# Layer 0's scores and search in four 32-row quarters, each search pair inside the scores; expert stages by chunks

## The reference

```
x = x + tanh(g_xattn[0]) * L0_xattn(layernorm(x), ctx)
x = x + tanh(g_ffn[0])   * L0_ffn(layernorm(x))
x = x + tanh(g_xattn[1]) * L1_xattn(layernorm(x), ctx, mask)
x = x + tanh(g_ffn[1])   * L1_ffn(layernorm(x))

L0_xattn:  q = query @ Wq.T in 32 heads of 4;  k = ctx @ Wk.T likewise;  v = ctx @ Wv.T in 16 heads of 8
           a1, a2 = softmax(q1 k1^T / 2) v, softmax(q2 k2^T / 2) v      (heads 0-15 and 16-31)
           attn = a1 - lam * a2;  attn *= rsqrt(mean(attn^2) + 1e-5) * subln_w * (1 - LAMBDA_INIT)
           out = attn @ Wp.T + bp
L1_xattn:  the plain one, 16 heads of 8, with biases, masked scores set to the least float
L0_ffn:    softmax over 8 experts, the two best, weighted: silu(x @ w_up.T) @ w_down.T, plus a shared expert
L1_ffn:    the two best of 8, softmax over the two: (silu(h1) * h2) @ w3.T
```

## Time and profile before

| | |
|---|---|
| median of 3 runs | 2283.0 us (2277.94 to 2285.57) |
| the profiled execution | 2273.94 us, its span 2272.1 us |
| PE busy | 2036.9 us, 90% |
| DVE busy | 1702.4 us, 75% |
| ACT busy | 1497.4 us, 66% |
| POOL busy | 1273.1 us, 56% |
| exponentials of 896 columns, L1081 | 1152 of 915 ns |
| reductions of 500 keys, L1139 | 1536 of 672 ns |

### The profile page before, as it was taken

One profiled execution on the slowest core, in us unless ns is written; L12 is line 12 of the kernel. 1 busy time (PEld: TensorE's weight loads), 2 busy tenths in 40 slices (PEclk: granted clock), 3 DMA queues, 4 the chain that ended last, 5 costly groups with the idle time before them and its releaser, 6 DMA issues. The chain is left out here.

```text
span 2272.1 us, 67374 instructions
## 1 busy us (share of the span) xinstructions
PE 2036.9 (90%) x27256; PEld 1260.1 (55%) x27256; DVE 1702.4 (75%) x3701; ACT 1497.4 (66%) x2101; POOL 1273.1 (56%) x1418
## 2 busy tenths in 40 slices
PE   3799999999999999999985985999999999998798
PEld 2344444444444444444443863567766776676576
DVE  3688888888888888888943554777777777774644
ACT  2168888888888888888773432577777777776322
POOL 5326556556556556556423444687777778771332
PEclk9589999999999999999997996799999999999799
DMA  3544453453443443444301015677767777761000
GB/s 101 129 84 109 93 112 108 95 112 107 95 112 107 95 112 107 95 112 108 67 2 54 25 31 120 141 157 146 155 140 147 154 153 152 144 141 37 33 1 16
DMA packets 95244, 227.82 MB, mean 100 GB/s; under 512 B 46308, under 2 KB 58852, under 8 KB 88292
## 3 DMA queue, kind: packets, MB, share of 16 engines
q1 hardware_dynamic: 94692, 223.67, 44.2%
q10 hardware_dynamic: 256, 0.00, 0.0%
HBM read 146.77 MB, written 76.48 MB: 98 GB/s over the span
## 5 line engine op out<-in xcount | busy, mean ns | idle before, releaser
L1081 ACT ACTIVATE probs<-score_ps 125x896 f32<-125x896 f32 x1152 | 1039.0, 915 | 309.4 <-PE score_ps L978 304.7
L1139 DVE TENSOR_REDUCE max_part<-max_ps 112x1 f32<-112x500 f32 x1024 | 663.6, 672 | 81.8 <-PE max_ps L949 43.0
L995 PE MATMUL acc_ps<-probs,vext 125*32 125x224 f32 (+1 forms) x12288 | 563.4, 312 | 4.5 <-issue 3.7
L978 PE MATMUL score_ps<-qstack,kstack 50*125 50x224 f16 (+1 forms) x6144 | 456.2, 249 | 72.4 <-ACT probs L1081 67.1
L978 PEld LDWEIGHTS score_ps<-qstack,kstack 50*125 50x125 f16 x6144 | 305.5, 134 | 310.5 <-ACT probs L1081 246.5
L949 PE MATMUL max_ps<-kstack,qstack 48*112 48x500 f16 x1536 | 460.5, 394 | 17.8 <-DMA kstack<-k_parts 12.9
L995 PEld LDWEIGHTS acc_ps<-probs,vext 125*32 125x32 f32 x12288 | 303.4, 110 | 188.8 <-issue 136.3
L1136 DVE CUSTOM_DVE_ANT_0 kstack<-max_ps,kstack 112x500 f32<-112x500 f32 x512 | 333.4, 675 | 84.1 <-PE max_ps L949 56.0
L1139 DVE TENSOR_REDUCE max_part<-spare_ps 112x1 f32<-112x500 f32 x512 | 344.5, 673 | 44.6 <-PE max_ps L949 42.9
L949 PE MATMUL spare_ps<-kstack,qstack 48*112 48x500 f16 x768 | 304.4, 396 | 18.7 <-issue 16.8
L1136 DVE CUSTOM_DVE_ANT_0 kstack<-spare_ps,kstack 112x500 f32<-112x500 f32 x256 | 172.8, 675 | 83.9 <-PE max_ps L949 80.9
(11 more groups left out here) (187 smaller groups left out, 2617.5 us busy)
## 6 DMA issues: line engine op xcount, KB each, us to landing
kstack<-k_parts SPq DMA_DIRECT2D x384, 187.5 KB, 6.4
k_parts<-khl SPq DMA_DIRECT2D x128, 375.0 KB, 2.9
ctx_f<-in_ctx SPq DMA_DIRECT2D x32, 750.0 KB
ctx_f<-context_parts SPq DMA_DIRECT2D x22, 750.0 KB, 8.0
context_parts<-ctx_f SPq DMA_DIRECT2D x16, 750.0 KB, 3.3
context_parts<-kstack SPq DMA_DIRECT2D x16, 750.0 KB, 3.3
mask_in<-in_mask SPq DMA_DIRECT2D x128, 82.0 KB
XnT<-context_parts SPq DMA_DIRECT2D x10, 750.0 KB, 8.2
```

The costliest lines, as they stand in the source:

```text
L978: last = nc.tensor.matmul(buf[0:KT, r, GC * k:GC * (k + 1)], kstack[n % SLOTS][rows, c, keys], qstack[n % SLOTS][rows, c, :], start=not L. ...
L995: last = nc.tensor.matmul(acc_ps[32 * j:32 * j + 32, TT * S * i:TT * S * (i + 1)].rearrange("p (s c) -> p s c", s=S), vext[n % SLOTS][:, c ...
L1081: nc.scalar.activation(probs[t % 2][:, 896 * h:896 * h + 896].rearrange("k (b c) -> k b c", b=2), score_ps[h][0:KT, :, 0:448], ACT.Exp, sc ...
L1139: nc.vector.reduce_max(best, scores, AX.X).then_inc(s_red, 1)
```

## The change

Layer 0's stacks are four quarters of 32 partitions (`TILE`, `ROW_TILES`) with 8 dimensions to a group: 24 rows and the two of ones and maxima make 26. A matmul of `scores` takes 26 rows and gives 112 columns; place 0 uses two of the quarters and place 1 the other two. Search has 24 rows. `piece` orders the pairs so that each takes the two quarters that the scores beside it don't, and `scores` issues the pair ahead of its first matmul (`SEARCH_AT = 0`). Layer 0 has one order of a step. All DMAs that fill or load stacks in layer 0 are for each quarter, so twice as many. Layer 1 keeps its halves. In `feed_forward` the loop over chunks is written out, the router's matmuls are split around the first expert's hidden units, the choice of experts and its exponential come later, the total of chunk c-1 is added in chunk c, and layer 1's result is stored by chunk in the same block.

```diff
-L0 = Layer("L0", 32, 4, False)
-L1 = Layer("L1", 16, 8, True)
+L0 = Layer("L0", 32, 4, False, HALF // 2)
+L1 = Layer("L1", 16, 8, True, HALF)
...
-    CONST = 16 * (2 * SLOTS + (2 if L.masked else 0))
-    K_INC = 16 * 6
-    Q_INC = 16 * 6
-    M_INC = 16 * 4
+    CONST = 16 * (ROW_TILES * SLOTS + (2 if L.masked else 0))
+    K_INC = 16 * 3 * ROW_TILES
+    Q_INC = 16 * 3 * ROW_TILES
+    M_INC = 16 * 2 * ROW_TILES
+    SEARCH_AT = 0
...
-              "pairs apart by preparation": ("scores 0", "weigh", "scores 1", "pair 0", "prepare", "pair 1")}
+              "each search pair inside the scores": ("scores and pair 0", "weigh", "scores and pair 1", "prepare")}
     def order_of(n, t):
+        if not L.masked:
+            return ORDERS["each search pair inside the scores"]
...
     def piece(p):
-        r, third, c, i = p % 2, p // 2 % NTHIRD, p // (2 * NTHIRD) % PAIRS, p // (2 * NTHIRD * PAIRS)
-        return r, third, c, i, (r * PAIRS + c) * L.parts + i
+        if L.masked:
+            r, third, c = p % 2, p // 2 % NTHIRD, p // (2 * NTHIRD)
+        else:
+            turn = p // 4
+            r, third, c = 2 * (p // 2 % 2 ^ turn % 2) + p % 2, turn % NTHIRD, turn // NTHIRD
+        return r, third, c, r * PAIRS + c
...
             def fill_k(n):
                 at_least(sp, s_scores, (n - 2) * STEPS * 2)
                 for part, blocks in ((0, (0, 1)), (1, (2,))):
                     sp.wait_ge(s_kd[part], 16 * (n + 1))
                     for k in blocks:
-                        for r in range(2):
-                            row = HALF * r + GD * k
+                        for r in range(ROW_TILES):
+                            row = TILE * r + GD * k
                             sp.dma_start(kstack[n % SLOTS][row:row + GD, :, :],
-                                         T["k_dram"][n:n + 1, part, HALF * r:HALF * r + HALF, :]
+                                         T["k_dram"][n:n + 1, part, TILE * r:TILE * r + TILE, :]
                                          .rearrange("b (d c) k -> (b d) c k", c=PAIRS)).then_inc(s_ks[n % SLOTS], 16)
             def fill_m(n):
...
-                    for r in range(2):
-                        row = HALF * r + KROWS + part
+                    for r in range(ROW_TILES):
+                        row = TILE * r + KROWS + part
                         sp.dma_start(qstack[n % SLOTS][row:row + 1, :, :].rearrange("a c q -> a (c q)"),
-                                     max_rows[half * r:half * (r + 1), part, 0:PIECE]).then_inc(s_mrow[n % SLOTS], 16)
+                                     max_rows[groups * r:groups * (r + 1), part, 0:PIECE]).then_inc(s_mrow[n % SLOTS], 16)
...
-            def scores(n, t, place):
+            def scores(n, t, place, pair=()):
...
-                for k, c in enumerate(columns):
-                    for r in range(2):
-                        rows = slice(HALF * r, HALF * r + KROWS + 2)
-                        last = nc.tensor.matmul(buf[0:KT, r, GC * k:GC * (k + 1)], kstack[n % SLOTS][rows, c, keys],
+                for c in range(PAIRS):
+                    if c == SEARCH_AT and pair:
+                        search(pair)
+                    for b in range(2):
+                        r = 2 * h + b if H == 2 else b
+                        rows = slice(TILE * r, TILE * r + KROWS + 2)
+                        last = nc.tensor.matmul(buf[0:KT, b, GC * c:GC * (c + 1)], kstack[n % SLOTS][rows, c, keys],
                                                 qstack[n % SLOTS][rows, c, :], start=not L.masked, stop=True,
                                                 skip_group_check=True)
...
         def steps(eng, body):
-            body(0)
-            with eng.Fori(1, NCH) as c:
+            for c in range(NCH):
                 body(c)
...
             def chunk(c):
                 for e in range(NX):
                     up(c, e)
+                    if c == 0 and e == 0:
+                        route(range(FIRST_ROUTED, NTT))
                     if e:
                         down(c, e - 1)
                 down(c, NX - 1)
+            route(range(FIRST_ROUTED))
...
-            act.wait_ge(s_d, 1)
-            nc.scalar.activation(m[:, 3, :], m[:, 2, :], ACT.Exp).then_inc(s_e, 1)
             def chunk(c):
                 for u in range(NX * NF):
                     number = c * (NX * NF) + u
+                    if number == 2 * NF:
+                        act.wait_ge(s_d, 1)
+                        nc.scalar.activation(m[:, 3, :], m[:, 2, :], ACT.Exp).then_inc(s_e, 1)
...
+                    if c == 0 and e == 0:
+                        choose_experts()
+                    if c == 0 and e == 1:
+                        weigh_experts()
                     if e:
                         take(c, e - 1)
+                    if c and e == 2:
+                        add_total(c - 1)
```

More of the change, by code:

```diff
@@ L594, in order_of @@
             return ORDERS["both scores first"]
-        if L.masked and not busy[0]:
-            return ORDERS["scores apart by a pair"]
-        return ORDERS["scores apart by the product" if L.masked and busy[0] else "scores apart by the product" if busy[0] else "scores apart by the product"]
+        return ORDERS["scores apart by the product" if busy[0] else "scores apart by a pair"]
     turnaround = [("F", i) for i in range(L.uses_f)] + [("A", 0)]
@@ L1027, in _ @@
                             scores(n, t, int(work[-1]))
+                        elif work in ("scores and pair 0", "scores and pair 1"):
+                            scores(n, t, int(work[-1]), searched(n, t, int(work[-1])))
                         elif work in ("pair 0", "pair 1"):
@@ L1188, in expert_weights, with feed_forward @@
     return up, down
-def feed_forward(T, layer):
+def feed_forward(T, layer, out=None):
     nc, a, sem, bank, X, XnT, small = T["nc"], T["a"], T["sem"], T["bank"], T["X"], T["XnT"], T["small"]
@@ L1226, in feed_forward @@
     AHEAD = 2
+    FIRST_ROUTED = 6
     def makes_parts(c, e):
-        if not isinstance(c, int):
+        if c:
             return [], []
@@ L1260, in _ @@
                         sp.dma_start(mask_row[t], src[:, CH * c + t, :]).then_inc(s_mask, 16)
+        if layer == 1:
+            s_out = sem("result_stored")
+            @block.sync
+            def _(sp):
+                for c in range(NCH):
+                    sp.wait_ge(s_res, c + 1)
+                    sp.dma_start(out[CW * c:CW * c + CW, :].rearrange("(t p) d -> p t d", p=TT),
+                                 X[:, CH * c:CH * c + CH, :]).then_inc(s_out, 16)
+                sp.wait_ge(s_out, 16 * NCH)
         def before_hidden(c, u):
@@ L1273, in _, with route @@
         def _(pe):
-            for t in range(NTT):
-                last = nc.tensor.matmul(bank[7][0:TT, NE * t:NE * t + NE], XnT[:, TT * t:TT * t + TT],
-                                        small[f"routerT{layer}"][:, :], start=True, stop=True)
-            last.then_inc(s_lg, 1)
-            pe.wait_ge(s_w, 32)
+            def route(tiles):
+                for t in tiles:
+                    last = nc.tensor.matmul(bank[7][0:TT, NE * t:NE * t + NE], XnT[:, TT * t:TT * t + TT],
+                                            small[f"routerT{layer}"][:, :], start=True, stop=True)
+                if t == NTT - 1:
+                    last.then_inc(s_lg, 1)
             def project(ps, c, e, row):
@@ L1350, in chunk @@
                     else:
-                        if not (isinstance(c, int) and number < HS):
+                        if number >= HS:
                             act.wait_ge(s_dn, before_hidden(c, u))
```

144 lines of the change are left out of this document (68 added, 76 removed).

## The result

The changed kernel takes 2431.7 us in the median of 4 runs (2412.43 to 2444.82), the kernel before 2281.7 in the 4 runs beside it: ratio 1.065, 95% interval 1.056 to 1.074. The forecast was 2345 with a range of 2250 to 2395. The direction is right, the size isn't: 150 us more instead of 62.

The account below looks back on a forecast made before the run. PE bounds one slot of a step, the scores-exponential loop the other. Key waits +51.9, start +14, tail +7.8 and expert stages -11.6 sum to +62 on the median 2283.0: 2345 us, range 2250 to 2395.

Parts of the forecast that it names:

- What bounds, and the expert stages: PE or the scores-exponential loop bounds alternate slots; expert stages, with store and layer 0's end, save 11.6 us.
- The store: End of layer 1's expert stage: storing by chunk leaves a quarter of the 5.4 us store, -1.6 us.
- The start: Before layer 0's first search: extra ones-row and query DMAs and a later first fill cost 14 us, bounds 3 to 14.
- The quarters on PE, 2.72 a step: Layer 0's attention: slots of 1.27 and 1.45 us, a step of 2.72 against 2.84, a batch 32.64 us.
- The key fill: Layer 0: twelve 8-row DMAs at 61 GB/s land 21.1 us after first issue; step 7 waits 3.2 us a batch.
- The maxima: Layer 0's batch start: eight DMAs instead of four give a period of 33.1 to 36.0, taken 34.8, hidden under 35.84.
- What I charged for the waits: Layer 0's 30 batches with a fill: period 35.84, 1.73 over 34.11, +51.9 us in the sum.
- rival 1: Layer 0: key wait plus falling clock, or rate under 61; period 37, +103 us, 2386; chance 0.15.
- The tail, +7.8: Batches 30 and 31, without search: steps of 2.71 instead of 2.23 us, +7.8 us, ends 0 and +20 (half clock).
- rival 2: Layer 0: no overlap on PE, step 3.02, period 36.2 without key wait; +106 us, 2389; chance 0.08.
- rival 4: Layer 0: neither transfer binds, start costs 5, PE's saving comes through; -43 us, 2240; chance 0.23.

Follow-up runs that it names:

- the run with the fills reordered: Changed kernel with layer 0's twelve key fills issued for quarters 0, 2, 1, 3 instead of 0, 1, 2, 3: 2376.5 us.
- both transfers mended: Changed kernel with key fills issued for quarters 0, 2, 1, 3 and the eight DMAs of the maxima made two: 2328.3 us.
- The tail mended alone: Changed kernel with both scores first in steps without a search pair, from step 7 of batch 30 on: 2376.4 us.
- the pair behind in place 1: Changed kernel with fills reordered, two maxima DMAs, both scores first without a pair, and place 1's search pair behind its scores: 2277.5 us, ratio 0.998.
- the run with the late fill: Kernel before, with the key fill of batch n+2 issued only after 8 score places of batch n: 2325.1 us against 2280.1, ratio 1.020.

## Why the prediction was wrong

- *What bounds, and the expert stages*: right. The two stages and the store gave -10.8 of -11.6 in the changed kernel, 12 alone. The store saved more than its term, 2.9 us (5.4 to 2.5) for 1.6, so the other terms gave less.
- *The start*: right, +14.3 for +14.
- *The quarters on PE, 2.72 a step*: the slot of pair and scores right (1.26 for 1.27). The other was 1.55 for 1.45, inside its bounds of 1.32 to 1.58: I put it at the low end since the pair goes first. But the pair delays the last scores, hence the exponential, by 0.1 us. 12 x 0.09 = 1.1 us a batch.
- *The key fill*: its mechanism right. 8 engines, 70 GB/s for the 61 taken, a median of 20.4 us for the 21.1 to landing. The wait at step 7 was 0.8 to 4.3 us in 22 of 30 batches, for 3.2 in each.
- *The maxima*: right as a second limit, at the forecast's 34.8, which the run with the fills reordered shows. That the number is exact is in part luck: it was picked between 33.1 and 36.0, and in the batch shown the first DMA goes 28.8 us in, not 28.3, and the eighth 4.3 behind it, not 4.8.
- *What I charged for the waits*: this is the step that failed. The sum has 30 x 1.73 = 52 us for a period at full clock; half clock behind the waits stands at nothing in it. It stood only in rival 1, with one stretch a batch and at most 1.2 us. There were 161 us of it in batches 0 to 29, against 9 before, and these batches cost 103 us more. What a stretch costs can be read where little else varies: with the fills reordered, batches with 1, 2, 3 and 5 stretches of 3.4 us take 35.9, 36.9, 38.2 and 39.8 us for 34.9, about 1 us for each. By this 152 us more at half clock are some 45 us (an estimate), close to the 51 that the term lacked. The other 58 are near the 52 of the sum: the batches without half clock and long wait take 34.8 (21 us over 34.1), 12.7 are the stops inside products, which the sum didn't have, and some 24 are left for the key waits.
- *What shows that the waits are behind it*: with both transfers mended (and the step still 2.81) batches 0 to 29 take 1040.8 us instead of 1127.4, with 54 us of half clock instead of 161. Waits and clock together are 87 of the 103 us; some 31 of the 87 are clock by the same estimate.
- *The tail, +7.8*: failed in the same way, +30.2, with 70 of 86 us at half clock. The half clock was named as the upper end, +20, and I took the value at full clock; even the end was too low. The tail mended alone gave 25 back.
- *Rival 1* had the mechanism, a key wait and a falling clock, with a chance of 0.15. Its 2386 is still 46 short of 2431.7. In rival 2 one sum is off: 30 times the 2.1 between 36.2 and 34.1 is 64, not 61; nothing hangs on it.
- *The other side* (rival 4): what it said of PE's saving is real, 32.7 a batch, but only with the pair behind its scores, the fills in another order and the maxima in two DMAs. With the pair behind in place 1 the kernel is level with the one before: 7.6 us won in batches 0 to 29 of the profiled runs, 9.0 lost at the start, 5.4 in the tail, 12.5 won in the expert stages, 2.8 lost in layer 1; the median is 2277.5.

Left open: why a stop of 1.1 us brings half clock in some batches and not in others that look alike, why PE waits longer for ACT in step 1 (1.10 for 0.80), and what the stops inside a product wait for.

## What to carry to other kernels

A wait that you add to a PE which is nearly full has two prices, the wait and the clock behind it; where the trace shows one instance of the second, put it into the sum, and not only into a rival. When a layout cuts a transfer into twice as many pieces of half the rows, count the engines and the rate of a piece, not its bytes, and look for a strided form that keeps the number of pieces. And a change that carries five edits should be tried by parts: here the one that wins 12 us was hidden by those that lose about 150.

## What the runs showed of the hardware

- 16-row DMAs of 12 KB rows into the partitions moved 122 GB/s with all engines busy, 8-row ones 70 GB/s with half of them, and 81 when neighbours in the queue went to partitions 64 apart rather than 32. The same bytes took 11.0, 20.4 and 17.9 us from first issue to last landing.
- One DMA may write four single rows 32 partitions apart: two such took the place of eight, and SP's issue went from 4.91 us to 1.1:

```profile
615.30 1.11 SPq L700 DMA_DIRECT2D qstack<-max_rows  x2
```

- A scores product and a search product in different quarters of 32 rows started within 0.01 us and ran together; with the pair issued first, the exponential started 0.57 us behind the scores, with the scores first 0.48.
- The granted clock fell to 1.2 GHz for 3.4 us and multiples, in or behind stops of PE of 1.1 to 5.3 us. In the run with the late fill the six waits of 1.39 to 1.87 us brought it and the 23 of 0.60 to 1.39 didn't. In the quarters a stop of 1.10 us a batch left the clock at 2.4 GHz in 22 of 30 batches once the waits for transfers were gone.
